# Second and last cross attention: maxima in two halves per batch, exponentials 12 slots behind the scores

## What is computed

```python
x = x + cross_attention(layernorm(x), ctx)      # 16 heads of size 8, 256 queries, 512 keys, softmax
```

## Time and profile before

| | |
|---|---|
| median of 3 runs | 1242.35 us (1239.1 to 1244.07) |
| the profiled execution | 1246.88 us, span on the core 1245.6 us |
| TensorE busy | 1028.6 us (83%) |
| VectorE busy | 800.2 us (64%) |
| ScalarE busy | 612.5 us (49%) |
| mean granted TensorE clock | 0.867 |

### The profile page before, as it was taken

The page is one execution under the profiler, slowest core; times in us unless marked ns, Lnnn a source line. Parts: engine busy times, 40 slices in busy tenths (PEclk is TensorE's granted clock), DMA queues, the critical chain, the costliest instruction groups (busy, mean ns, idle before and its releaser), DMA issues.

```text
span 1245.6 us, 19903 instructions
## 1 busy us (share of the span) xinstructions
PE 1028.6 (83%) x7630; PEld 550.0 (44%) x7649; DVE 800.2 (64%) x2016; ACT 612.5 (49%) x1018; POOL 252.0 (20%) x309
## 2 busy tenths in 40 slices
PE   5777779999899974778867889999658868779999
PEld 4233313333667652345532333566412333437767
DVE  7786867751324467877777882677688887665412
ACT  2456436566433527678763777323115546433342
POOL 2833210000000225477551000001222001000000
PEclk9778869999999996566776997999858989879999
DMA  8323040000000210068013201700101200100000
GB/s 302 94 72 85 27 179 2 2 2 2 1 1 1 77 54 7 1 186 156 17 45 125 116 2 19 125 1 1 52 26 33 97 1 2 34 1 1 1 9 9
DMA packets 34785, 61.23 MB, mean 49 GB/s; under 512 B 4771, under 2 KB 25076, under 8 KB 33092
## 3 DMA queue, kind: packets, MB, share of 16 engines
q1 hardware_dynamic: 33828, 58.64, 16.7%
q10 hardware_dynamic: 864, 1.33, 0.3%
HBM read 42.91 MB, written 16.65 MB: 48 GB/s over the span
## 4 chain that ended last, share of the span: by engine, by line
PE 59%; DVE 27%; ACT 5%; issue 4%; POOL 3%; DMA 2%; SPq 1%; DVEq 0%; POOLq 0%; ACTq 0%
PE ps_s L879 10%; PE ps_e L869 9%; PE ps_v L672 6%; DVE mx L1864 6%; PE ps_e L608 5%; PE ps_s L629 3%; PE ps_e L606 3%; DVE ps_s L1860 2%; PE ps_e L973 2%; PE ps_s L960 2%; ACT work L1396 2%; DVE mx L1854 2%; DVE stats L1802 1%; DVE xn L1820 1%; PE ps_v L1144 1%
## 5 line engine op out<-in xcount | busy, mean ns | idle before, releaser
L1396 ACT ACTIVATE work<-ps_e 128x512 f32<-128x512 f32 x448 | 250.7, 598 | 148.1 <-PE ps_e L608 142.8
L2622 POOL TENSOR_TENSOR rstd<-rstd,halves 128x2 f32<-128x2 f32 x52 | 36.6, 704 | 699.0 <-DVE rstd L1807 698.8
L1864 DVE TENSOR_REDUCE mx<-ps_s 128x2 f32<-128x1024 f32 x128 | 154.1, 1222 | 27.8 <-PE ps_s L629 26.3
L629 PE MATMUL ps_s<-ctx_stack,q_stack 49*128 49x512 bf16 (+1 forms) x384 | 128.5, 453 | 47.1 <-DVE mx L1864 34.8
L608 PE MATMUL ps_e<-q_stack,ctx_stack 52*128 52x256 bf16 (+1 forms) x768 | 149.7, 297 | 16.8 <-issue 6.3
L1498 ACT ACTIVATE work<-ps_s,keep 128x512 f32<-128x512 f32 x136 | 93.1, 687 | 140.4 <-PE ps_s L879 137.5
L672 PE MATMUL ps_v<-work,vaug 128*32 128x256 f32 x1536 | 132.0, 420 | 4.8 <-ACT work L1384 4.8
L869 PEld LDWEIGHTS ps_e<-ffn_w,work 128*128 128x128 f32 x960 | 117.9, 196 | 21.0 <-issue 19.9
L879 PE MATMUL ps_s<-xnT,ffn_w 128*128 128x512 f32 x240 | 119.4, 623 | 3.6 <-ACT work L1498 3.6
L869 PE MATMUL ps_e<-ffn_w,work 128*128 128x128 f32 x960 | 119.7, 280 | 0.8 <-DVE x L2054 0.8
L2064 DVE SCALAR_TENSOR_TENSOR x<-ps_e,gates,x 128x128 f32<-128x128 f32 x128 | 38.9, 346 | 121.7 <-PE ps_e L869 118.7
(11 more groups left out here) (380 smaller groups left out, 1815.7 us busy)
## 6 DMA issues: line engine op xcount, KB each, us to landing
q_stack<-q_scr SPq DMA_DIRECT2D x32, 192.0 KB
ffn_w<-in_L0f_w SPq DMA_DIRECT2D x1, 4608.0 KB, 14.7
ffn_w<-in_L1f_w SPq DMA_DIRECT2D x1, 3456.0 KB, 13.1
q_scr<-parts SPq DMA_DIRECT2D x16, 192.0 KB, 2.1
c_scr<-ffn_w SPq DMA_DIRECT2D x12, 256.0 KB, 7.7
kx_scr<-ffn_w SPq DMA_DIRECT2D x12, 256.0 KB, 4.2
ctx_stack<-kx_scr SPq DMA_DIRECT2D x2, 1536.0 KB
ctx_stack<-c_scr SPq DMA_DIRECT2D x2, 1536.0 KB
```

The source lines that it names most:

```text
L629: return pe.matmul(ps_s[i][:, parity, :], q_stack[p0:p0 + n_rows, b, pair, part * P:(part + 1) * P], ctx_stack[p0:p0 + n_rows, pair, b * S ...
L1396: act.activation(pt[:, parity, :, :].rearrange("p k q -> p (k q)"), bank[f"e{parity}"], ACT.Exp).then_inc(exped, 1)
L1864: m = dve.tensor_reduce(mx[:, b, :, pair, part], ps_s[i][:], AX, ALU.max, negate=True)
```

## The change

For `X1` and `X2` the maxima of a batch are split, turned and written in two halves of 8 steps each (four head pairs), so that there are 8 groups for each use instead of 4; `mparts` holds two halves side by side. `LEAD` goes from 20 to 12 for both. `EARLY_X1` goes from 16 to 8. All that hangs on a use's last slots (`close_slot`, routing, first units of `L1f` and `L3f`) comes 8 slots earlier. `X0`, the first cross attention, keeps groups of 16 steps.

```diff
-LEAD = {A0: 12, X0: 20, X1: 20, X2: 20}
+HALVED = (X1, X2)
+LEAD = {A0: 12, X0: 20, X1: 12, X2: 12}
 PERIOD = {A0: 8, X0: 16, X1: 16, X2: 16}
 STEPS = {A0: 32, X0: 64, X1: 64, X2: 64}
 STEP0 = {A0: 0, X0: 32, X1: 96, X2: 160}
-BATCH0 = {A0: 0, X0: 4, X1: 8, X2: 12}
+MAX_STEPS = {A0: 8, X0: 16, X1: 8, X2: 8}
+MAX0 = {A0: 0, X0: 4, X1: 8, X2: 16}
...
+    return LEAD[use] + (9 + 8 * b if use == A0 else 20 + 16 * b)
+
+
+def max_group(use, k):
+    return k // 2 if use in HALVED else k
+
+
+def max_due(use, k):
+    b = max_group(use, k)
+    halved = [u for u in HALVED if MAX0[u] < MAX0[use]]
+    before = USE_ORDER.index(use) + len(halved)
+    return 32 * (before + (k % 2 if use in HALVED else 0) + 1)
...
-EARLY_X1 = 16
+EARLY_X1 = 8
 CLOSE_X1 = 4
 EARLY_X2 = 5
-TAIL1 = 86
+TAIL1 = 78
...
+ROUTE1F = ROUTE0 - 8
...
+    def half_parts(half):
+        flat = mparts[:].rearrange("p a s c -> p (a s c)")[:, 48 * half:48 * half + 48]
+        return flat.rearrange("p (a s c) -> p a s c", a=2, s=3)
...
-            if exps and h % PERIOD[use] == 0:
-                pe.wait_ge(d_maxrow[h // PERIOD[use]], 32 * (BATCH0[use] // 4 + 1))
+            if exps and h % MAX_STEPS[use] == 0:
+                k = h // MAX_STEPS[use]
+                pe.wait_ge(d_maxrow[max_group(use, k)], max_due(use, k))
...
-            if t % 16 == 1 and t > 1 and t < 80:
-                turn_max(use, (t - 17) // 16, tile)
+            k, rest = divmod(t - MAX_STEPS[use] - 1, MAX_STEPS[use])
+            if rest == 0 and 0 <= k < STEPS[use] // MAX_STEPS[use]:
+                turn_max(use, k, tile)
...
-            if t % PERIOD[use] == PERIOD[use] - 1:
-                split_max(use, b, n)
-
-        def split_max(use, b, n):
-            col = mx[:, b, :, :, :].rearrange("p a h q -> p a (h q)")
+            if t % MAX_STEPS[use] == MAX_STEPS[use] - 1:
+                split_max(use, t // MAX_STEPS[use], n)
+
+        def split_max(use, k, n):
+            b = max_group(use, k)
+            lo, hi, part = 0, 8, mparts[:]
+            if use in HALVED:
+                lo, hi, part = k % 2 * 4, k % 2 * 4 + 4, half_parts(k % 2)
+            col = mx[:, b, :, lo:hi, :].rearrange("p a h q -> p a (h q)")
             dve.wait_ge(maxed, n)
             if use == X0:
                 settle(dve.tensor_scalar(col, col, -1.0, None, ALU.mult))
-            settle(dve.tensor_copy(mparts[:, :, 0, :], col))
-            settle(dve.tensor_tensor(col, col, mparts[:, :, 0, :], ALU.subtract))
-            settle(dve.tensor_copy(mparts[:, :, 1, :], col))
-            dve.tensor_tensor(mparts[:, :, 2, :], col, mparts[:, :, 1, :], ALU.subtract).then_inc(max_split, 1)
-
-        def turned_max(use, b, tile):
+            settle(dve.tensor_copy(part[:, :, 0, :], col))
+            settle(dve.tensor_tensor(col, col, part[:, :, 0, :], ALU.subtract))
+            settle(dve.tensor_copy(part[:, :, 1, :], col))
+            dve.tensor_tensor(part[:, :, 2, :], col, part[:, :, 1, :], ALU.subtract).then_inc(max_split, 1)
...
-        def max_rows(use, b):
-            sp.wait_ge(max_T, BATCH0[use] + b + 1)
+        def max_rows(use, k):
+            b = max_group(use, k)
+            sp.wait_ge(max_T, MAX0[use] + k + 1)
+            lo, hi, rows = (k % 2 * 4, k % 2 * 4 + 4, 24) if use in HALVED else (0, 8, 48)
             for parity in range(2):
                 p0 = parity * SLOT + rows_of(use, b)[2]
-                sp.dma_start(q_stack[p0:p0 + 3, b, :, :].rearrange("s h (q t) -> s (h q) t", q=TPB),
-                             mT[parity * 48:(parity + 1) * 48, b, :]).then_inc(d_maxrow[b], 16)
+                sp.dma_start(q_stack[p0:p0 + 3, b, lo:hi, :].rearrange("s h (q t) -> s (h q) t", q=TPB),
+                             mT[parity * rows:(parity + 1) * rows, k % B, :]).then_inc(d_maxrow[b], 16)
...
-        for b in range(1, B):
-            max_rows(X1, b)
+        for k in range(1, 2 * B):
+            max_rows(X1, k)
...
         cross_inputs(X2, 0)
         cross_inputs(X2, 1)
         max_rows(X2, 0)
+        max_rows(X2, 1)
         cross_inputs(X2, 2)
-        max_rows(X2, 1)
+        max_rows(X2, 2)
+        max_rows(X2, 3)
         cross_inputs(X2, 3)
         sp.wait_ge(down_ps, down_at("L1f", NE, B - 1))
         sp.dma_start(ffn_w[:, 0:own], d["L3f_w"][:, 0:own]).then_inc(d_w3, 16)
-        max_rows(X2, 2)
-        max_rows(X2, 3)
+        for k in range(4, 8):
+            max_rows(X2, k)
```

More of the change, by code:

```diff
@@ L117 @@
 USE = {A0: 0, X0: 1, A1: 2, X1: 3, X2: 4}
+USE_ORDER = (A0, X0, X1, X2)
 OVERLAP = 36
@@ L151 @@
 PS_AT = order_of([(at, b) for _, b, at in sorted((close_slot(X2, b) + at, b, at) for at in CHAIN_PS for b in range(B))])
-LAST = {A0: 54, X0: 96, X1: 96, X2: 93, "chain": 125}
+LAST = {A0: 54, X0: 96, X1: 88, X2: 85, "chain": 117}
 CFILL = {X0: 32, X1: 128, X2: 192}
@@ L562, in project, with turn_max @@
             free["m"] = (proj_T, PROJ_AT[st, b])
-        def turn_max(use, b, tile):
-            n = BATCH0[use] + b + 1
+        def turn_max(use, k, tile):
+            n = MAX0[use] + k + 1
             i = tile()
             pe.wait_ge(max_split, n)
-            pe.transpose(ps_s[i][0:96, 0, 0:64].bitcast(BF16), mparts[:].rearrange("p a s c -> p (a s c)"),
+            src = half_parts(k % 2) if use in HALVED else mparts[:]
+            rows = 48 if use in HALVED else 96
+            pe.transpose(ps_s[i][0:rows, 0, 0:64].bitcast(BF16), src.rearrange("p a s c -> p (a s c)"),
                          ident_b[:]).then_inc(max_ps, 1)
@@ L1355, in tensor_program @@
             cross_slot(X1, t, kp("L1x_oT"), "L1f")
-            if t == ROUTE0:
+            if t == ROUTE1F:
                 route("L1f", kp("L1f_router"), 0, (0, 1), "m")
@@ L1772, in scalar_program @@
             cross_slot(X1, t, "L1f")
-            if t == ROUTE0 + 1:
+            if t == ROUTE1F + 1:
                 route("L1f", 0, slice(0, 4))
@@ L1873, in split_max, with turned_max @@
                 settle(dve.tensor_scalar(col, col, -1.0, None, ALU.mult))
-            settle(dve.tensor_copy(mparts[:, :, 0, :], col))
-            settle(dve.tensor_tensor(col, col, mparts[:, :, 0, :], ALU.subtract))
-            settle(dve.tensor_copy(mparts[:, :, 1, :], col))
-            dve.tensor_tensor(mparts[:, :, 2, :], col, mparts[:, :, 1, :], ALU.subtract).then_inc(max_split, 1)
-        def turned_max(use, b, tile):
-            i = tile()
-            if BATCH0[use]:
-                dve.wait_ge(d_maxrow[b], 32 * (BATCH0[use] // 4))
-            dve.wait_ge(max_ps, BATCH0[use] + b + 1)
-            dve.tensor_copy(mT[:, b, :], ps_s[i][0:96, 0, 0:64].bitcast(BF16)).then_inc(max_T, 1)
+            settle(dve.tensor_copy(part[:, :, 0, :], col))
+            settle(dve.tensor_tensor(col, col, part[:, :, 0, :], ALU.subtract))
+            settle(dve.tensor_copy(part[:, :, 1, :], col))
+            dve.tensor_tensor(part[:, :, 2, :], col, part[:, :, 1, :], ALU.subtract).then_inc(max_split, 1)
+        def turned_max(use, k, tile):
+            i = tile()
+            if k >= B:
+                dve.wait_ge(d_maxrow[max_group(use, k - B)], max_due(use, k - B))
+            elif MAX0[use]:
+                last = USE_ORDER[USE_ORDER.index(use) - 1]
+                if last in HALVED:
+                    dve.wait_ge(d_maxrow[max_group(last, B + k)], max_due(last, B + k))
+                else:
+                    dve.wait_ge(d_maxrow[k], max_due(last, k))
+            dve.wait_ge(max_ps, MAX0[use] + k + 1)
+            rows = 48 if use in HALVED else 96
+            dve.tensor_copy(mT[0:rows, k % B, :], ps_s[i][0:rows, 0, 0:64].bitcast(BF16)).then_inc(max_T, 1)
         def weigh(use, g, tile):
@@ L1986, in cross_slot @@
                 greatest(use, t, tile)
-            if t % 16 == 1 and t > 1 and t < 80:
-                turned_max(use, (t - 17) // 16, tile)
+            k, rest = divmod(t - MAX_STEPS[use] - 1, MAX_STEPS[use])
+            if rest == 0 and 0 <= k < STEPS[use] // MAX_STEPS[use]:
+                turned_max(use, k, tile)
             g, rest = divmod(t - LEAD[use] - 8, 4)
```

9 lines of the change are left out of this document (4 added, 5 removed).

## The result

The changed kernel took 1261.19 us in the median of 4 runs (1259.33 to 1266.79), the kernel before beside it 1243.21 us (4 runs, 1239.1 to 1245.88). The ratio is 1.015, with a 95% interval from 1.012 to 1.019: slower by 18 us, where 11.7 were forecast, and just above the range, which ended at 1261. The profiled execution took 1261.82 us, 14.9 above that of before.

A forecast was written before the change was run, and what follows sets the result against it. X1's slots with scores and exponentials were taken as bound by TensorE or VectorE, both nearly full, and X2's led by VectorE. X1 +12.3 and X2 -0.6 summed to +11.7 us: 1254 us against the 1242.35 median, range 1241 to 1261.

The forecast's parts named there:

- The wait in slot 20: X1: second half group's maxima queue behind 4528 KB of weights and mask on SyncE; +10.2 us, bounds 0.8 and 12.
- the rival that the queue does not hold the maxima: Slot 20 of X1: small DMAs overtake the weights, wait 0.8 us; sum +0.2 us, 1243; 12 in 100.
- routing product, which only moves: X1, eight slots of exponentials alone: 1.06 us of their 13.9 us, taken as only moving.
- X1's group ends: X1: more groups of maxima, +7.2 us; three new ends make 6.0, slot 15's end 1.2.
- The clock after the wait: X1, behind slot 20's wait: TensorE's clock low after idling; +2.1 us, bounds 0 and 5.6.
- Early stretches: X1: eight early slots go, two at each of four places; -5.8 us.
- Exponentials alone: X1: eight slots with exponentials alone give way to eight with both; -1.4 us.
- What vanishes: X2: the stretch of slots 64 to 71 goes; -17.5 us.
- Slots 12 to 20: X2: exponentials and sums move into slots 12 to 19, where VectorE is full; +2.5 us, bounds 0 and 5.
- Half groups: X2: four more group ends cost VectorE about 1.1 us each, DMAs hidden; +4.4 us.
- so I charge all 10: X2: chain of small steps falls 8 slots earlier, beside maxima; VectorE work charged fully, +10 us, bounds 0 and 12.
- The rival that idle time takes the chain: X2: VectorE's idle time absorbs the chain, the 10 us cost nothing; sum +1.7 us, 1244; 15 in 100.

The follow-up runs named there:

- q_spread: Changed kernel with SyncE's three large loads (L1f weights, L2f weights, mask) issued one by one behind the maxima of groups 1, 2, 3 of X1: 1253.01 us, ratio 1.008.
- x1_mended: Kernel before with X1 changed only, the three large loads spread behind groups of maxima and the L1f router back at slot 68: 1242.75 us, ratio 0.998.
- q_small: Changed kernel with only L2f weights and mask issued behind the second half group's maxima, L1f weights staying ahead: 1262.12 us, ratio 1.013.
- x1_only: Changed kernel with X2 put back as in the kernel before, so only X1 is changed: 1264.93 us, ratio 1.015.
- x1_r61: x1_mended with the L1f router in slot 61, beside the last maxima, instead of 68: 1247.48 us in a single execution.
- x1_mended_2: x1_mended run once more, unchanged, beside another kernel on one chip: 1242.79 us, ratio 1.000.
- x2_only: Changed kernel with X1 put back as in the kernel before, so only X2 is changed: 1245.0 us, ratio 1.002.
- x2_groups: x2_only with X2's lead of 20 and chain places of before, so only the half groups of X2 remain: 1248.03 us, ratio 1.005.
- mended: Changed kernel, X1 and X2 both changed, with the large loads spread behind the maxima and the L1f router at slot 68: 1246.86 us, ratio 1.002.

## Why the prediction was right and wrong

The direction, the mechanism that decides it and its place were right. The size was too small, 11.7 us for 18 by the medians. Two steps failed: the router's move in `X1` was put at nothing, and the chain beside `X2`'s maxima was priced too low. In `X1` most of the first was hidden: the group ends were 4.8 us too dear, and the profile of before held 4.0 us of low clock that after's did not. By the two profiled executions `X1` and `X2` miss by 2.8 and 7.0 us, together 9.8; that these executions differ by only 14.9 comes from 6.6 us in stretches where the code hardly differs, which the sum could not know.

**The wait in slot 20: right.** Forecast 23.5 us from slot 12 to 20, measured 23.2; the wait 10.2, by experiment 9.7 (after against q_spread) to 11.0 (against x1_mended, whose clock was higher there, 0.67 for 0.51). q_spread took it away, q_small took 3.2 us of it away with 1072 KB of 4528. So the rival that the queue does not hold the maxima falls. The two DMAs were asked for 1.6 us behind the mask, not 3, and that the issue itself would take 8.16 us was not foreseen. The landing came where it was forecast all the same: 686.1 - 664.0 = 22.1 us after slot 12, for 22.2. The Trainium skill (DMA: Bandwidth & Descriptors, Queues, rings and completion order) says that completion is not FIFO per issuing engine. The trace agrees, in a small way: the maxima were there at 680.97 + 5.13 = 686.1, while the mask, issued ahead of them at 671.18, landed 15.7 us later, at 686.9. Its row among the DMA issues of the kernel after:

```profile
self_stack<-in_mask_L SPq DMA_DIRECT2D x1, 512.0 KB, 15.7
```

**The router: the missing term.** The prediction gave the "routing product, which only moves" no price, since it looked at the 1.06 us of TensorE in the earlier trace rows. What moves with it are 22 small operations of VectorE, 4.7 us in one piece, from slots where VectorE is busy 7.0 of 13.9 us into slots where it is full (7.41 of 8.4 without the router). Between after and x1_mended that is 9.1 us where it lands, less 1.0 by which the last slots are shorter without it: +8.1. Some 2 of these go with the clock, 0.61 in after; at 0.78, in x1_only, it is 6.9 where it lands, and x1_r61 has 6.5. The prediction counted TensorE's row and not those on the engine that is the bound. For `X2` it did make that count.

**X1's group ends: too dear.** Charged were 7.2 us. Against before, x1_mended spent 3.2 us more in the 36 slots with three more ends. Part of that is the clock: its slots 20 to 28 took 13.9 us at 0.88, those of x1_mended_2 12.9 at 1.00. With x1_mended_2, at 1.00 in all 36 slots as before was, it is 61.3 against 59.0: 2.3 us, 0.8 for each end. In the first eight slots it was 0.1 for 1.2, at a clock of 0.67 for 0.59. Even the lower bound of 1.0, half a group each, was high; what of the 2.0 us in the earlier trace rows does not come a second time was not taken apart. This error hid more than half of the missing term.

**The clock after the wait: +1.7 for +2.1, nearly right.** Slots 20 to 56 took 63.0 us after and 61.3 in x1_mended_2, at full clock; after's clock was 0.50 from slot 20 on for 5.4 us (687.20 to 692.60). Against x1_mended, which had a fall of its own there, it is only 0.8. The larger effect of the clock came without the wait: in q_spread's profile slots 20 to 58 took 5 us more than in after, at 0.86 for 0.96.

**Early stretches: right.** -5.2 for -5.8.

**Exponentials alone: +1.1 for -1.4.** Eight such slots took 13.3 us in before and the eight that took their place 12.0 in x1_mended. That is -1.3 and looks like the forecast (whose own rows give 13.9 - 1.06 - 11.5 = 1.3, not 1.4), but by luck: the 13.3 us hold the router and the 12.0 do not, and the price was read at a clock of 0.77. x2_only has `X1` in its old form and ran these slots at 1.00:

```profile
741.90:753.50 11.60, 11.00 (x110) 4.23 (x111) 6.46 (x34) 9.11 (x20) 0.00 (x0) 1.00 0.02 5
753.50:768.90 15.40, 14.76 (x148) 5.27 (x148) 3.13 (x14) 13.09 (x27) 0.70 (x1) 1.00 0.01 1
```

The eight slots and the last twelve together are 27.0 us there and 28.1 in x1_mended, both with the router: the swap costs 1.1. Before took 31.0 for them, at a clock of 0.78: 4.0 more. Whether the change has a part in that fall of the clock is not shown; the old form had it in two profiles (0.75 in x2_groups for the first eight of these slots) and not in the third. `X1` in its old form took 149.5 us in before and 146.1 in x2_only, hardly more than what the two mended kernels took (144.8 and 146.1).

**X2: 3 to 5 us too hopeful.** By medians x2_only is +2.4 us (0 to 6) and mended 4.1 above x1_mended; in the profiles `X2` in its old form took 188.0 to 194.4 us (seven, mean 189.8) and in its new form 191.5 to 195.5 (six, mean 194.3). The forecast was -0.6. What vanishes was nearly right: from slot 64 to the end x2_only took 27.7 us for 43.9 before, -16.2 for -17.5. Slots 12 to 20 took 17.7 and, in after, 18.8 for 16.5: +1.2 and +2.3 for +2.5. Half groups cost 3.1 for 4.4, by single profiles. The term that failed is "so I charge all 10": the chain beside maxima cost 16.4, of which 11.6 is VectorE's work and 4.9 new waiting of VectorE. The work itself was 1.6 us above the 10; the upper bound of 12 left no room for the waiting. That a chain over three engines waits for its turn at each step beside work that fills VectorE is the likely reason and was not shown; the clock (0.82 for 0.84) may have a part in it. The rival that idle time takes the chain falls: idle time grew.

**Sum for `X1`:** -5.2 early, + 0.1 + 2.3 group ends, + 11.0 wait, + 1.7 clock behind it, + 1.1 exponentials, + 9.1 - 1.0 router, - 4.0 clock of before in its last 20 slots: +15.1, the table's sum.

## What to carry to other kernels

When work is moved in a schedule, list what moves on every engine, and price it on the engine that is full where it lands: a step of 1 us on TensorE drew 5 us of small VectorE operations with it, and cost 6 to 8. When a small transfer is wanted earlier, look at what was issued ahead of it on its queue; here 4.5 MB of weights and masks, the first of them needed some 60 slots later, cost 10 to 11 us, and with them behind the small ones no stretch shows a loss by it. An idle share of an engine need not be room for a chain of dependent steps: the chain here cost its whole work and two fifths more. And before a stretch's price is used, look at its clock in more than one execution: the same 20 slots of the same code took 31.0 us in one and 27.0 in another.
